# Attention stage of a two-layer kernel: x for the queries and the attention's output split into high and low parts in rows, and turned by transposing transfers

## What is computed

```python
q = rms_norm(x @ Wq + bq, gq).reshape(b, -1, 16, 32)         # x: layer-normed residual
k = rms_norm(ctx @ Wk_img + bk_img, gk_img).reshape(b, -1, 16, 32)
v = (ctx @ Wv_img + bv_img).reshape(b, -1, 16, 32)
scores = einsum('bqnd,bknd->bnqk', q, k) / sqrt(32)
out = einsum('bnqk,bknd->bqnd', softmax(scores), v)
x = x + out.reshape(b, -1, 512) @ Wo + bo
```

## Time and profile before

| | us |
|---|---|
| median of three runs | 1194.92 |
| lowest, highest | 1192.79, 1200.13 |
| the profiled execution | 1189.34 |
| its span, first to last instruction | 1187.6 |
| TensorE busy in the span | 1052.3 (89%) |
| VectorE | 886.2 (75%) |
| ScalarE | 699.8 (59%) |
| GpSimd | 612.2 (52%) |

### The profile page before, as it was taken

The page is one execution under the profiler, slowest core; times in us unless marked ns, Lnnn a source line. Parts: engine busy times, 40 slices in busy tenths (PEclk is TensorE's granted clock), DMA queues, the critical chain, the costliest instruction groups (busy, mean ns, idle before and its releaser), DMA issues. The chain is left out here.

```text
span 1187.6 us, 25080 instructions
## 1 busy us (share of the span) xinstructions
PE 1052.3 (89%) x9286; PEld 781.8 (66%) x9375; DVE 886.2 (75%) x1634; ACT 699.8 (59%) x1103; POOL 612.2 (52%) x629
## 2 busy tenths in 40 slices
PE   5899997688888899958899998798998899999995
PEld 5677776633333567727777776497775788888873
DVE  5589998977777798667888888498975455655638
ACT  4565773667777556548788877285454254554530
POOL 4444445635546332338788888322686255555510
PEclk9999998889999999969999999857999799999998
DMA  8683531067777312331222220095696477678978
GB/s 306 196 252 120 159 90 63 1 188 189 192 192 181 126 46 93 98 94 41 56 58 56 55 55 11 22 389 200 161 261 238 145 242 243 232 244 283 310 264 299
DMA packets 117184, 191.45 MB, mean 161 GB/s; under 512 B 51360, under 2 KB 53558, under 8 KB 116140
## 3 DMA queue, kind: packets, MB, share of 16 engines
q1 hardware_dynamic: 100732, 146.26, 39.4%
q0 software_dynamic: 8544, 24.68, 6.7%
q10 hardware_dynamic: 7792, 18.96, 5.1%
HBM read 128.49 MB, written 44.47 MB: 146 GB/s over the span
## 5 line engine op out<-in xcount | busy, mean ns | idle before, releaser
L470 PE MATMUL ps_y<-kv,toep 128*128 128x288 f32 x640 | 157.0, 407 | 2.6 <-DMA toep<-taps_padded 1.4
L470 PEld LDWEIGHTS ps_y<-kv,toep 128*128 128x128 f32 x640 | 121.0, 190 | 38.1 <-DMA toep<-taps_padded 3.7
L1647 POOL TENSOR_TENSOR vw<-at_pf,kw 128x1024 bf16<-128x1024 f32 x64 | 136.5, 2133 | 2.7 <-ACT kw L1707 2.7
L164 POOL TENSOR_TENSOR kv<-kx 128x1024 f32<-128x1024 f32 x32 | 60.6, 1893 | 83.8 <-DVE outT L524 35.4
L2633 POOL DMA_INDIRECT expert_results<-e_yo,target x47 | 69.1, 1469 | 57.9 <-ACT e_yo L2680 57.9
L1703 ACT ACTIVATE at_pf<-ps_st 128x1024 f32<-128x1024 f32 x64 | 65.5, 1023 | 40.3 <-PE ps_st L1843 36.2
L1092 PE MATMUL ps_fY<-w2T,f_qbT 128*128 128x512 bf16 x253 | 61.0, 395 | 22.2 <-DVE x_res L926 18.5
L1754 DVE TENSOR_REDUCE at_negmax<-ps_s 128x4 f32<-128x1024 f32 x64 | 78.4, 1225 | 2.8 <-PE ps_s L1804 0.9
L1123 PEld LDWEIGHTS ps_eg<-e_xT,e_w 128*128 128x128 bf16 x1128 | 68.5, 100 | 14.7 <-issue 2.6
L1123 PE MATMUL ps_eg<-e_xT,e_w 128*128 128x128 bf16 x1128 | 72.7, 222 | 3.4 <-DVE e_xT L2741 3.4
L1123 PE MATMUL ps_eu<-e_xT,e_w 128*128 128x128 bf16 x1128 | 72.7, 222 | 0.0
(11 more groups left out here) (463 smaller groups left out, 3088.8 us busy)
## 6 DMA issues: line engine op xcount, KB each, us to landing
e_parts<-down_parts SPq DMA_DIRECT2D x47, 512.0 KB, 4.2
w_raw<-in_L_ffn_w ACTq DMA_DIRECT2D x32, 512.0 KB, 4.2
toep<-taps_padded SPq DMA_DIRECT2D x32, 256.0 KB, 3.6
f_draw<-in_L_ffn_rw SPq DMA_DIRECT2D x16, 512.0 KB, 4.3
down_parts<-f_dparts SPq DMA_DIRECT2D x16, 512.0 KB, 2.9
expert_weights<-expert_results SPq DMA_DIRECT2D x16, 512.0 KB, 10.3
x_res<-in_x SPq DMA_DIRECT2D x4, 1024.0 KB, 11.7
c_in<-in_ctx SPq DMA_DIRECT2D x4, 1024.0 KB, 14.4
```

Source lines behind the costliest of these rows:

```text
L164: pool.tensor_tensor(pairs[:, :, :, 0:HD0], x[:, :, 0:HD0].unsqueeze(2).broadcast_to([P, ROWS_N, WIDE, HD0]), sliding_rows(x, 0, 1, WIDE), ...
L470: last = pe.matmul(y[:, l * B:(l + 1) * B, :, WIDE - 1:], toep[h % 2][:, (DC - 1 - l + m) * P:(DC - l + m) * P], kv[h % 2][:, m * B:(m + 1 ...
L1647: pool.tensor_tensor(pl[u % 4][:, :, :, :], pf[u % 2][:, :, :, :], ph[u % 4][:, :, :, :], ALU.subtract)\
```

## The change

The PSUM turns of x and of the output (but for the last batch) go. Instead ScalarE rounds the normalised x, as rows, in one instruction of 128x1024 into `at_xrows`, and VectorE subtracts from the same SBUF tile into the low half of `at_xrows`; SP issues two transposing transfers (128 rows, 1024 columns) from there to `at_xT`, from which TensorE reads. The output goes the same way over `at_orows` and `at_oT`. The normalisation of x moves from step 1 to step 0, its split from steps 2 and 3 to step 1; the split of the output from step 7 of batch c+1 to step 3 (for batch 6 from (7, 4) to (7, 2)). The turn and split of batch 7 stay as they were. The projections stay at their steps; the first of a tile now also waits until the tile of the batch before is added. `spread` has one wait less.

```diff
-        xn = two("at_xn", [P, D], F32)
-        x_hi, x_lo = ahead.source
+        xn = sb("at_xn", [P, TPB, D], F32)
+        x_rows, o_rows = (sb(f"at_{n}rows", [P, TPB, 2, D], BF16) for n in "xo")
+        xT, oT = (sb(f"at_{n}T", [P, TPB, 2, DC, P], BF16) for n in "xo")
+        x_hi, x_lo = (lambda kc: xT[:, :, 0, kc, :]), (lambda kc: xT[:, :, 1, kc, :])
...
-        def turn_step(c):
-            return (c + 1, 7) if c < B - 2 else (B - 1, 4) if c == B - 2 else (B, 2)
+        LAST_TURN = (B, 2)
+        TURN_INCS = 16 * TPB
+
+        def split_step(c):
+            return (c + 1, 3) if c < B - 2 else (B - 1, 2)
...
+                if u == 1 and queried(b + 2):
+                    n = nth(b + 2)
+                    sp.wait_ge(x_low, n + 1)
+                    if n:
+                        sp.wait_ge(q_psum, n * DC)
+                    for t in range(TPB):
+                        sp.dma_start_transpose(xT[:, t, :, :, :].rearrange("p h c t -> p (h c) t"),
+                                               x_rows[:, t, :, :].rearrange("p h d -> p (h d)")).then_inc(xT_loaded, 16)
+                for c in range(B - 1):
+                    if (b, u) == split_step(c):
+                        sp.wait_ge(o_low, c + 1)
+                        for t in range(TPB):
+                            if c:
+                                sp.wait_ge(y_psum, (c - 1) * TPB + t + 1)
+                            sp.dma_start_transpose(oT[:, t, :, :, :].rearrange("p h c t -> p (h c) t"),
+                                                   o_rows[:, t, :, :].rearrange("p h d -> p (h d)")).then_inc(oT_loaded[t], 16)
...
-            def x_highs(q, t):
-                act.wait_ge(xt_psum, q * TPB + t + 1)
-                act.activation(x_hi[:, :, t * P:(t + 1) * P], psP[0][:, :].rearrange("p (c t) -> p c t", c=DC), ACT.Copy)\
-                   .then_inc(x_high, 1)
...
+            def x_highs(n):
+                act.wait_ge(xn_ready, (n + 1) * TPB)
+                if n:
+                    act.wait_ge(xT_loaded, n * TURN_INCS)
+                act.activation(x_rows[:, :, 0, :], xn[:, :, :], ACT.Copy).then_inc(x_high, 1)
+
+            def o_highs(c):
+                act.wait_ge(o_read, (c + 1) * G)
+                if c:
+                    for t in range(TPB):
+                        act.wait_ge(oT_loaded[t], 16 * c)
+                act.activation(o_rows[:, :, 0, :], o[c % 2][:, :, :], ACT.Copy).then_inc(o_high, 1)
...
-            def x_lows(q, t):
-                dve.wait_ge(x_high, q * TPB + t + 1)
-                half = slice(t * P, (t + 1) * P)
-                dve.tensor_tensor(x_lo[:, :, half], psP[0][:, :].rearrange("p (c t) -> p c t", c=DC), x_hi[:, :, half],
-                                  ALU.subtract).then_inc(x_low, 1)
+            def o_lows(c):
+                dve.wait_ge(o_high, c + 1)
+                dve.tensor_tensor(o_rows[:, :, 1, :], o[c % 2][:, :, :], o_rows[:, :, 0, :], ALU.subtract).then_inc(o_low, 1)
+
+            def x_lows(n):
+                dve.wait_ge(x_high, n + 1)
+                dve.tensor_tensor(x_rows[:, :, 1, :], xn[:, :, :], x_rows[:, :, 0, :], ALU.subtract).then_inc(x_low, 1)
...
-                if u in (2, 3) and queried(b + 2):
-                    x_lows(nth(b + 2), u - 2)
+                if u == 1 and queried(b + 2):
+                    x_lows(nth(b + 2))
...
-                if u in (2, 3) and queried(b + 2):
-                    turn_x(b, nth(b + 2), u - 2)
+                if (b, u) == LAST_TURN:
+                    turn_last_out()
...
-                    pe.wait_ge(x_low, q * TPB + 2)
+                    pe.wait_ge(xT_loaded, (q + 1) * TURN_INCS)
+                    if b >= 2:
+                        pe.wait_ge(y_added, (b - 2) * TPB + 1)
```

More of the change, by code:

```diff
@@ L1665, in biased_and_squared, with normalised @@
                 act.activation(sq[:, c, :], psP[c % 2][:, 0:S], ACT.Square, bias=bias).then_inc(squared, 1)
[L1667 to L1670 removed]
+            def normalised(q):
+                act.wait_ge(shift_ready, 1)
+                if nth(q):
+                    act.wait_ge(x_low, nth(q))
+                for t in range(TPB):
+                    tile = q * TPB + t
+                    act.activation(xn[:, t, :], xtile(tile), ACT.Identity, bias=x_shift[:, tile:tile + 1],
+                                   scale=x_rstd[:, tile:tile + 1]).then_inc(xn_ready, 1)
@@ L1672, in _ @@
             for b, u in STEPS:
                 g = b * G + u
[L1674 to L1679, removed]
-                if u == 1 and queried(b + 2):
[L1681 to L1685, removed]
+                for c in range(B - 1):
+                    if (b, u) == split_step(c):
+                        o_highs(c)
@@ L1686, in _ @@
+                if (b, u) == following(LAST_TURN):
+                    for t in range(TPB):
+                        act.wait_ge(ot_psum, t + 1)
+                        act.activation(oT[:, t, 0, :, :], psP[t][:, :].rearrange("p (c t) -> p c t", c=DC), ACT.Copy)\
+                           .then_inc(ot_high, 1)
+                if u == 0 and queried(b + 2):
+                    normalised(b + 2)
+                if u == 1 and queried(b + 2):
+                    x_highs(nth(b + 2))
                 if u == 2 and queried(b + 1):
@@ L1845, in transposed_scores @@
                 last.then_inc(st_psum, 1)
[L1847 to L1855, removed]
+            query_sum = lambda c: psP[c % 2][:, 0:S].rearrange("p (t q) -> p t q", t=TPB)
             def query_highs(c, chunks):
@@ L1865, in query_lows @@
                 for kc in range(DC):
-                    last = pe.matmul(psP[c % 2][:, 0:S], qw[:, 0, kc, cols], x_lo[:, kc, :], start=False, stop=(kc == DC - 1))
+                    last = pe.matmul(query_sum(c), qw[:, 0, kc, cols], x_lo(kc), start=False, stop=(kc == DC - 1))
                 last.then_inc(q_psum, 1)
@@ L1904, in project @@
                 for d in (2 * h, 2 * h + 1):
-                    last = three_products(pe, psP[t][:, :], [a[:, d, t * P:(t + 1) * P] for a in (o_hi, o_lo)],
+                    last = three_products(pe, psP[t][:, :], [oT[:, t, part, d, :] for part in range(2)],
                                           [ow[:, s, d, :] for s in range(2)], False, d == DC - 1)
```

48 lines of the change are left out of this document (23 added, 25 removed).

## The result

| kernel | us, median (lowest to highest) | ratio to before, 95% interval |
|---|---|---|
| before | 1193.86 (1191.95 to 1200.13) | |
| after | 1222.6 (1220.04 to 1224.35) | 1.0236 [1.0206, 1.0265] |

The account below looks back on a forecast made before the run. It took VectorE to bound steps 0 to 2 and GpSimd step 4, despite TensorE's 28.2 of 28.9 us. Batch terms 13.8 + 2.4 + 0.6 + 0.1 + 2.4 = 19.3 us gave 1213 us, range 1198 to 1227 (8 in 10).

Parts of the forecast that it names:

- VectorE is where it is decided: New subtractions after x's and the output's rounding: 1.23 us alone, but held by GpSimd to about 2.9 and 2.1 us.
- steps 0 to 4: One batch worked through from its step-7 copy at 636.94: copies at 639.8, 644.15, 649.85, 652.7, 658.5; batch 3.45 us longer.
- Transfers hidden: SP's four transposing transfers per batch: two land within 6.8 us, with over 8 us to spare, so they cost nothing.
- The gain of TensorE: PSUM turns of output and x leave TensorE: 2.0 us per batch of 28.9, at most 0.56 us of step 7 kept.
- The rival that they come back: TensorE's saved time returns in steps 7, 2 and 3: 1182 us, or 1188 with half; a gain had chance 0.08.
- The sign of 25 to 26 us of busy time: If right, TensorE is busy 25 to 26 us of a 32.3 us batch, waiting before the products of steps 3 and 4.
- Batches 2 to 5: Batches with both splits and the projections: 3.45 us longer each, 13.8 us together.
- Batch 1: Both splits without added tiles: 1.2 us for x at step 2, second split as in later batches; 2.4 us.
- Batch 6: Output only: maxima kept back behind at_qlo cost 0.8 (1.2 less 0.4 won in step 1), step 7 gains 0.7; 0.1 us.
- Batch 7: Split in step 2 held by GpSimd's vw: 2.8 us less 0.4 of slack, 2.4 us; the turn going there gains nothing.
- a rival with a chance of 0.17: TensorE's clock halves after its pause before the query products: up to 1.75 us a batch, 10 over six, 1224 us; chance 0.17.
- the likeliest case: Both subtractions held by GpSimd, clock mostly full: 1207 to 1221 us, chance 0.5.

Follow-up runs that it names:

- psum_operand: The changed kernel with both new VectorE subtractions taking their second input from a PSUM column instead of SBUF: 1210.16 us, ratio 1.0206.
- x_alone: The kernel before with x alone split in rows and turned by transfers, the output still turned by TensorE: 1204.48 us, ratio 1.0145.
- the filler kernel: The changed kernel with unused TensorE products put into its idle time to keep the clock up: 1208.92 us, ratio 1.0183.

## Why the prediction came out as it did

- **VectorE is where it is decided: right.** The subtractions took 2.82 and 1.98 us at the places named (2.9 and 2.1 had been worked out), the maxima waited behind the second (1.20 us at 669.00), and batch 2 took the 32.3 us of the sum. That the lock is the cause, and not the work, is shown from both sides: without the second SBUF input 2.6 of 3.4 us vanish; with it alone the kernel before loses 2.4.
- **Steps.** From the step-7 copy (649.30 after, 636.94 before), steps 0 to 4 were worked out at 2.9, 7.2, 12.9, 15.8 and 21.6 us; measured 3.0, 7.5, 13.1, 16.1 and 21.6. Of the 0.56 us that were to be left of the output's turn at step 1, 0.3 came (7.47 for 7.77 us from copy 7 to copy 1). The scalings of q were at fault: they began at 655.09, 0.47 us late, since TensorE's product that spreads the norms (L1912) stands behind the projection of step 0 (row at 655.09), a wait that the prediction didn't have. Step 3 was 0.3 shorter than worked out, so that the two errors cancel: that step 4 came to the tenth is luck.
- **Transfers hidden: right.** They landed in 3.1 to 4.9 us (6.8 allowed for two), and taking them out changed nothing. The price per transposed block that the Trainium skill gives (VectorE: DVE Perf Modes, The three transpose paths) never came onto the path; one issue of 128x1024 took 1.3 us of SP.
- **The gain of TensorE: right that it stays unused.** Its 2 us per batch became waiting (15.0 us of waits for the maxima at its products, for 4.4). The rival that they come back is out. The sign of 25 to 26 us of busy time missed: 28.9 were counted, 1.4 of them by the low clock (4.34 for 2.98 us in step 3); psum_operand, whose steady batches run at 1.00, has 26.8.
- **The sum, term by term.** Batches 2 to 5: 13.8 forecast, 18.0 measured. Batch 0: 0.6, 0.9. Batch 1: 2.4, 2.4. Batch 6: 0.1, 1.3. Batch 7: 2.4, 4.8. Together 19.3 and 27.4. The term that was mis-sized is the clock: the sum holds nothing for it, and it stood only in a rival with a chance of 0.17, as up to 10 us over six batches. It cost 1.1, 1.4 and 1.6 us in batches 3, 4 and 5 (up to 1.75 each had been worked out), and nothing in batch 2, though the clock was low for 3.4 us there too: that stretch, 599.1 to 602.5, lay in step 3, whose length GpSimd's at_qlo and the held maxima set (5.46 us, as 5.53 in batch 4 at full clock). In batches 3 to 5 it lay on the query products. The kernel x_alone has the same twice, in step 3 of batches 4 and 5 (the first shown here), and its batches take 31.63 and 31.64 us like the two with full clock:

```profile
663.00:666.40 3.40, 3.40 (x21) 1.56 (x17) 2.54 (x6) 0.29 (x1) 3.40 (x2) 0.52 0.58 127
```

- **Batch 1.** That its 2.4 us agree is in part luck: the steps with the two subtractions cost 1.0 and 1.1 us, step 0 0.3 and step 5 0.9, and the turn that went from step 7 gave 0.9 back, which the sum for this batch didn't count.
- **Batch 7.** The split in step 2 cost 2.5 us, where 2.4 were forecast, and step 0 another 0.5. Step 5 took 6.0 us instead of 3.3 with the clock at 0.50 from 763.0 to 769.8, while step 4, from which the turn of batch 6's output went, won 0.9. The two steps together take 7.4 us before, 9.2 in the changed kernel and 7.2 in the filler kernel at full clock, so that some 2 us of batch 7 are the clock. Its meeting with GpSimd has no part in them: step 5 takes 6.8 us at 0.51 in psum_operand too.
- **Batch 6.** Its step 7 lost 0.7 us as forecast, and the maxima behind at_qlo cost 1.1 us for the 1.2 of the forecast. What failed is the gain of 0.4 us that I set against it: step 0 is 0.55 us longer, and step 4, at a mean clock of 0.52, 0.3.
- **The size.** The direction and the meetings were right, but 1222.6 us lies outside the 1207 to 1221 that the likeliest case was given, and nearest to the rival in which the clock falls too (1224); it lies inside the whole range because that rival was in it. What it had wrong is the spread: some 4 us came in batches 3 to 5 and 2 in batch 7, where it had up to 1.75 in each of six batches. Of the 8.1 us missed in the attention part 4.4 are what batches 3 to 5 take over batch 2, 2.4 batch 7, 1.2 batch 6 and 0.3 batch 0; the steady meetings themselves came out 0.2 below the sum (13.6 for 13.8). The predicted 1213 us are 9.6 below the measured; the remaining 1.5 us are of the size by which runs of one kernel differ.

## What to carry to other kernels

When work is moved from one engine to another, ask of each new VectorE operation whether both inputs are in SBUF, and what GpSimd does in that very microsecond: the same subtraction was worth 1.2 or 2.8 us by its place alone, and the kernel with both of them moved, by five steps and by two, gave back 19.5 of 28.6 us. Freeing the busiest engine (98% here) gained nothing, since its waits lay in a loop that others closed; worse, an idle TensorE then met its next products at half the clock, which is a second price and is added to the first. Ask also what starts only when a divided operation has its last part: the halves of at_qlo made the maxima earlier and the scores wait for transfers. Check the first and last rounds of a pipeline apart: the versions whose steady batches were as short as before or shorter lost 2 to 7 us in the first and last ones.

## What was not expected of the hardware

- The lock between VectorE and GpSimd goes both ways, and the one that comes second stands still: a VectorE subtraction of 1.22 us took 2.82 against a running vw of 2.13, and a GpSimd addition of 0.22 us took 1.20 to 1.25 against a running subtraction. At 669.00 VectorE, which had waited since 668.15, went before GpSimd's next operation in its queue. The Trainium skill (SBUF — State Buffer, Who interferes with whom) has the contention and says that the order of issue decides who blocks. The rows agree, 2.82 us one way round and 1.20 to 1.25 the other; what they add is that an operation that already stands still comes before the next one of the engine that runs.
- A stretch of 3.4 us at the lower clock cost nothing in batch 2 and 1.1, 1.4 and 1.6 us in batches 3 to 5. In batch 2 it began some 12.5 us after the first copy of the batch, where another engine set the step, in the others 17.8 to 18.7 us after it, on TensorE's own products.
